# Attention rows of q and k packed into 81 partitions, and the rows of the maxima written by GpSimd's DMAs

## What is computed

```python
mod = silu(c) @ w_adaln + b_adaln            # 6 parts: shift, scale, gate, twice
h   = ln(x) * (1 + scale) + shift
q, k, v = split(h @ w_qkv + b_qkv)           # 16 heads of 9 columns
attn = softmax(q @ k.T * 9 ** -0.5)
x = x + gate * ((attn @ v) @ w_proj + b_proj)
...                                          # layer 0: experts, layer 1: an MLP, with their own ln and gate
```

## Time and profile before

| | |
|---|---|
| median of 3 runs | 464.79 us (460.39 to 464.89) |
| the profiled execution's own time | 465.79 us |
| its span, first to last instruction | 463.9 us |
| PE, DVE, ACT, POOL busy | 84%, 69%, 47%, 18% of the span |
| mean granted TensorE clock | 0.937 of full |

### The profile page before, as it was taken

One profiled execution on the slowest core, in us unless ns is written; L12 is line 12 of the kernel. 1 busy time (PEld: TensorE's weight loads), 2 busy tenths in 40 slices (PEclk: granted clock), 3 DMA queues, 4 the chain that ended last, 5 costly groups with the idle time before them and its releaser, 6 DMA issues.

```text
span 463.9 us, 5953 instructions
## 1 busy us (share of the span) xinstructions
PE 390.6 (84%) x1938; PEld 167.9 (36%) x1938; DVE 321.0 (69%) x837; ACT 216.8 (47%) x428; POOL 85.7 (18%) x95
## 2 busy tenths in 40 slices
PE   1616592689999999899999998998998999998897
PEld 0102220112333332337676663651332333322464
DVE  7797283989889888352716852789797788881653
ACT  1113320157777668752243333124676677687421
POOL 5999945990000000000000000000000000000000
PEclk9999955569999999999999999996999999999999
DMA  6000775124741300000000024300023300000001
GB/s 171 1 0 9 177 182 132 34 81 126 205 131 50 81 1 3 0 1 0 2 0 1 0 76 128 104 2 0 1 70 114 102 27 2 0 3 0 1 0 52
DMA packets 19470, 24.05 MB, mean 52 GB/s; under 512 B 5652, under 2 KB 16088, under 8 KB 19116
## 3 DMA queue, kind: packets, MB, share of 16 engines
q1 hardware_dynamic: 15008, 21.47, 16.4%
q0 software_dynamic: 3040, 1.62, 1.7%
q10 hardware_dynamic: 1392, 0.59, 0.4%
HBM read 19.38 MB, written 4.14 MB: 51 GB/s over the span
## 4 chain that ended last, share of the span: by engine, by line
PE 62%; DVE 16%; DMA 8%; issue 5%; SPq 4%; ACT 4%; DVEq 0%; ACTq 0%
PE bank L1243 12%; PE bank L1121 12%; PE bank L1258 10%; PE bank L1267 8%; PE bank L1221 8%; DVE nmax L938 6%; DMA Qs<-qk_parts 4%; SPq L475 2%; PE bank L1168 2%; DMA qk_parts<-prob 2%; ACT prob L1072 2%; PE bank L1285 2%; PE bank L1224 2%; DVE mpart L739 2%; DMA w<-in_L_cond_b_adaln_dram 1%
## 5 line engine op out<-in xcount | busy, mean ns | idle before, releaser
L938 DVE TENSOR_REDUCE nmax<-bank 128x1 f32<-128x512 f32 x256 | 165.2, 682 | 35.9 <-PE bank L1258 35.1
L1072 ACT ACTIVATE prob<-bank 128x512 f32<-128x512 f32 x256 | 135.5, 602 | 44.1 <-PE bank L1267 43.5
L1258 PE MATMUL bank<-Ks,Qs 96*128 96x512 bf16 x256 | 103.9, 419 | 19.6 <-DMA Qs<-qk_parts 13.1
L1267 PE MATMUL bank<-Qs,Ks 98*128 98x512 bf16 x256 | 98.3, 397 | 5.4 <-ACT prob L1072 4.2
L1121 PE MATMUL bank<-prob,Va 128*32 128x512 f32 x512 | 71.7, 633 | 0.2
L1258 PEld LDWEIGHTS bank<-Ks,Qs 96*128 96x128 bf16 x256 | 25.1, 100 | 91.6 <-DVE nmax L938 48.7
L1243 PE MATMUL bank<-w,big 128*128 128x144 f32 (+1 forms) x320 | 52.5, 305 | 0.2
L1061 ACT ACTIVATE big<-bank 128x512 f32<-128x512 f32 (+1 forms) x46 | 27.0, 597 | 47.0 <-PE bank L1224 46.9
L1243 PEld LDWEIGHTS bank<-w,big 128*128 128x128 f32 (+1 forms) x320 | 42.6, 188 | 10.6 <-DVE y L904 2.6
L1267 PEld LDWEIGHTS bank<-Qs,Ks 98*128 98x128 bf16 x256 | 25.2, 100 | 36.9 <-ACT prob L1072 16.5
L1221 PE MATMUL bank<-hTb,w 128*128 128x512 f32 x72 | 37.0, 594 | 0.0
(11 more groups left out here) (155 smaller groups left out, 452.6 us busy)
## 6 DMA issues: line engine op xcount, KB each, us to landing
Ks<-qk_parts SPq DMA_DIRECT2D x30, 108.0 KB
Qs<-qk_parts SPq DMA_DIRECT2D x90, 36.0 KB
qk_parts<-prob SPq DMA_DIRECT2D x6, 384.0 KB, 4.7
Ks<-qk_parts SPq DMA_DIRECT2D x6, 324.0 KB
Qs<-qk_parts SPq DMA_DIRECT2D x18, 108.0 KB
mod<-modulation SPq DMA_DIRECT2D x5, 288.0 KB, 4.1
w<-in_L_cond_w_dram SPq DMA_DIRECT2D x3, 432.0 KB, 5.4
w<-in_L_cond_w_dram SPq DMA_DIRECT2D x4, 288.0 KB, 3.6
```

Of the source, the lines that this page charges most:

```text
L938: V.tensor_reduce(nmax[:, half, odd * NT + k:odd * NT + k + 1], bank[:, :], AX.X, ALU.max, negate=True).then_inc(s_free, 1)
L1072: A.activation(probs[:, k % 2, j, :], bank[:, :], ACT.Exp, scale=SCALE).then_inc(t_free, 1)
L1258: M.matmul(bank[:, :], Qs[b][0:MROW, h_, k4 * P:(k4 + 1) * P], Ks[b][0:MROW, h_, :], start=True, stop=True).then_inc(s_full, 1)
L1267: M.matmul(bank[:, :], Ks[b][0:SROWS, h0 + k4, k * P:(k + 1) * P], Qs[b][0:SROWS, h0 + k4, :], start=True, stop=True).then_inc(t_full, 1)
```

## The change

- **Rows.** MROW becomes 81: the two rows of the maxima and of ones follow the parts at once (SROWS = 83), there are no zero rows, and all fills of GpSimd for Qs and Ks go away, with the semaphore `buf_ready`. The matmuls are 81 and 83 rows deep.
- **Ones.** DVE sets two partitions of `prob` to one (`onesb`), and two DMAs of ACT's queue spread them over rows 81, 82 of Ks[0] and Ks[1] (64 KB in all). ACT waits for both (`ones_in`) before stage qkv of n = 0.
- **Order of rows.** The rows of Ks are in the order (column, part), and Qs' are at stride 3, so that a piece takes 3 DMAs for Qs with 27 partitions each in place of 9.
- **Pieces.** Batch 0 has three pieces: heads 0 to 3, 4 to 7, 8 to 15.
- **Buffers.** `qkf[1]`, `qkp[1]` lie in Qs[1] in place of prob, so that ACT doesn't wait for `qk_out[0]` before qkv of n = 1, and the first slot waits for `qk_out[0]`, not `qk_out[1]`.
- **Maxima.** For n = 0 the 8 DMAs of mT stay on SP, the other 24 go to GpSimd's queue, behind all its splits.
- **GpSimd.** Va[1] is filled at the start, behind the loads for qkv0. The splits are cut into steps of at most 576 columns (HID).
- **Stages.** ("ada", 1, 0) moves ahead of the first qkv, and (1, 1), (1, 2) and the second turn behind it.

```diff
-MROW = 96
+MROW = PAIRS
...
-    s = [("ada", 0, 0), ("ln", 0, 0), ("ada", 0, 1), ("ada", 0, 2), ("turn", 0, 0, "a"), ("ln", 0, 1),
-         ("qkv", 0, 0, 0, QKV), ("turn", 0, 1, "a"), ("ada", 1, 0), ("ada", 1, 1), ("qkv", 0, 1, 0, QKV), ("ada", 1, 2)]
+    s = [("ada", 0, 0), ("ln", 0, 0), ("ada", 0, 1), ("ada", 0, 2), ("turn", 0, 0, "a"), ("ada", 1, 0),
+         ("ln", 0, 1), ("qkv", 0, 0, 0, QKV), ("ada", 1, 1), ("ada", 1, 2), ("turn", 0, 1, "a"), ("qkv", 0, 1, 0, QKV)]
...
-PIECES = (((0, G), (G, NH)), tuple((h, h + G) for h in range(0, NH, G)))
+PIECES = (((0, G), (G, 2 * G), (2 * G, NH)), tuple((h, h + G) for h in range(0, NH, G)))
...
+def m_landed(pair):
+
+    return (pair % 4, 16 * (pair // 4 + 1)) if 2 * pair < NH else (pair % 4, 16 * ((pair - NH // 2) // 4 + 1))
...
+        onesb = prob[0:MPARTS, 0:N // 2].bitcast(BF16)
+
         qkf, qkp = [], []
-        for place in (prob, prob, prob, big):
+        for place in (prob, Qs[1][:, :, :].rearrange("p h n -> p (h n)").bitcast(F32), prob, big):
...
                     lo, hi = PIECES[b][piece]
-                    width, cols, done = (hi - lo) * N, slice(lo * N, hi * N), qk_in[n][piece]
-                    src = parts[1].rearrange("j (d h) n -> (j d) (h n)", h=NH)[:, cols]
-                    for r in range(0, PAIRS, HD * PARTS):
+                    cols, done = slice(lo * N, hi * N), qk_in[n][piece]
+                    src = parts[1].rearrange("j (d h) n -> d j (h n)", h=NH)[:, :, cols]
+                    for i_ in range(PARTS):
+                        r = HD * PARTS * i_
                         sp.dma_start(Ks[b][r:r + HD * PARTS, lo:hi, :], src).then_inc(done, 16)
-                    for i_ in range(PARTS):
-                        src = parts[0, i_].rearrange("(d h) n -> d (h n)", h=NH)[:, cols]
-                        for r in range(HD * PARTS * i_, HD * PARTS * (i_ + 1), HD):
-                            sp.dma_start(Qs[b][r:r + HD, lo:hi, :], src).then_inc(done, 16)
+                    src = parts[0].rearrange("i (d h) n -> (i d) (h n)", h=NH)[:, cols]
+                    for j in range(PARTS):
+                        sp.dma_start(Qs[b][j:PAIRS:PARTS, lo:hi, :], src).then_inc(done, 16)
...
             load_raw("qkv0")
+            link(G_.memset(Va[1][:, :, :, :], 0.0))
+            G_.memset(Va[1][:, :, :, HD:HD + 1], 1.0).then_inc(v_ready[1], 1)
...
-            for k, (name, last) in enumerate((("proj0", "gate"), ("w1", "w1"), ("qkv1", "fc1"))):
-                a = WCOLS[name][0]
-                split_weights(a, sum(WCOLS[last]) - a).then_inc(w_split, 1)
+            for name, last in (("proj0", "gate"), ("w1", "w1"), ("qkv1", "fc1")):
+                a, end = WCOLS[name][0], sum(WCOLS[last])
+                for at in range(a, end, HID):
+                    done = split_weights(at, min(HID, end - at))
+                done.then_inc(w_split, 1)
+
+            for i, stage in enumerate(SCHED):
+                pair = turns_pair(stage)
+                if pair is not None and 2 * pair >= NH:
+
+                    n, h = 2 * pair // NH, 2 * pair % NH
+                    pool.wait_ge(t_free, T_AT[i + 1])
+                    if n >= B:
+                        pool.wait_ge(t_full, scores_ended(n - B))
+                    pool.dma_start(Qs[n % B][MROW:SROWS, h:h + 2, :], mT[:, pair % 2, :]).then_inc(m_pool[pair % 4], 16)
...
+            act.wait_ge(ones_ready, 1)
+            for b in range(B):
+                act.dma_start(Ks[b][MROW:SROWS, :, :],
+                              onesb.unsqueeze(1).to_broadcast([MPARTS, NH, N])).then_inc(ones_in, 16)
...
-                    if n and first == 0:
+                    if n == 0:
+                        act.wait_ge(ones_in, 16 * B)
+                    if n > 1 and first == 0:
                         act.wait_ge(qk_out[n - 1], 4 * 16)
...
-                        act.wait_ge(qk_out[1 if n0 == 0 else B], 4 * 16)
+                        act.wait_ge(qk_out[n0], 4 * 16)
```

35 lines of the change are left out of this document (13 added, 22 removed).

## The result

The kernel with the change takes 440.12 us (median of 4, 439.02 to 443.79), the kernel before in the same session 463.45 us (460.39 to 464.89): ratio 0.9519, 95% interval 0.9438 to 0.9599. So the change gains 23.3 us where 34 were forecast, and 440 lies at the upper edge of the range. The profiled execution took 441.05 us with a span of 439.2, 24.7 less than before.

A forecast was written before the change was run, and what follows sets the result against it. Before the slots, DVE and GpSimd's fills shut each other out, then waits followed; the slots were PE-bound. Terms -16.0 + 1.2 - 2.0 - 1.9 - 7.9 - 5.0 - 2.5 = -34.1 us gave 431 us, range 423 to 441.

The forecast's parts named there:

- Fills and ones: Without GpSimd's fills, qkv of n = 0 starts at 23.1 us, not 39.17: -16.0; loading the ones costs +1.2.
- Parts to DRAM: In layer 0, the parts' way to DRAM takes 5.0 us, not 7.0, with GpSimd's weight loads mostly over: -2.0.
- First piece: First piece of n = 0 takes 5.3 us, not 7.2, with six issues in 2.15 us: -1.9.
- the term for the transfer: In the first piece, 3.7 us for 648 KB at 175 GB/s, plus 1.0 until first packet and 0.6 at the end.
- Layer 1: PE's waits for first pieces of n = 2 and n = 3 each lose 0.9 to 1.3 us, clock dip partly spared: -2.5.
- Second piece and mpart: Layer 0: smaller pieces remove the second piece's wait, -7.9; shorter GpSimd splits cut waits of DVE's mpart casts, -5.0.
- GpSimd's 24 DMAs at nothing: Maxima pairs on GpSimd's queue land 2.2 us after 0.5 us issues, within the 4.2 us margin: no cost.
- rival 1: Maxima on GpSimd's queue reach the slots late: some late, 437 us, chance 0.10; all late, 487 us, chance 0.03.
- Rival 2: Backlog of the nine DMA engines delays the first slot's maxima to 64 us: +3, so 434 us; chance 0.12.
- Rival 3: New copy shapes use three engines, not nine, so a piece takes 11 us: 456 us; chance 0.03.
- Rival 4: PE stays at the high clock through layer 0's units and first slots: 425 us; chance 0.17.

## Why the prediction was wrong in size

- **Fills and ones: right.** -14.8 forecast, -16.1 at qkv. The two runs on the fills show both cause and size. PE's first product came at 10.27 and not 9.86, and at 9.89 to 10.47 in the other runs, which all write the ones; so these cost 0 to 0.6 of the 1.2 allowed.
- **Parts to DRAM: right** (-2.0, -2.4).
- **First piece: the step that failed.** "Six issues take 2.15" took 0.36 us an issue from the plain rows and gave it to copies of another shape; they take 0.69 to 0.75 each, 4.7 to 5.0 us for six. The first piece of n = 0 got 0.2 us longer in place of 1.9 shorter. The run with the first Q copies on a second queue shows that even with issues of 2.3 us it is 5.9 to 6.8 and not 5.3, so the term for the transfer was too small as well.
- **Layer 1: the same step, and the clock.** -2.5 forecast, +2.7 measured: 5.2 of the 9.4 us. The first piece of n = 2 takes 7.2 us and not 6.1 (279.50 to 285.58 before), that of n = 3 7.0 and not 6.6, so that the waits grew by 1.0 and 0.5 us where 0.9 to 1.3 were to go from each. The longer wait of n = 2 is followed by a low clock (0.72 from 260 to 266) that the kernel before did not have there (1.7 us of lead), and that of n = 3 by a longer one than before (1.5). With plain rows the piece of n = 2 took 1.2 us less, and the fall behind it was gone; but at the first slots the low clock was then 10 us long and not 3.4, and the lead won by it was lost again.
- **The first slots of layer 1: luck.** No term held them. The clock falls there in every kept trace: for 3.4 us in that of the changed kernel, for about 7 in four runs and for about 10 in the kernel before and in the other fourteen. The 2.0 us of lead that came back there stand in the 24.7, and no run shows that the change brings them.
- **Second piece and mpart: right in sum** (-12.9 forecast; the lead grows from 17.4 to 29.9), but the first has the wrong cause. The prediction gave -7.9 to the pieces of 4, 4 and 8; the runs give 1.3 to 1.9 to them and the rest to the fills. The splits are worth 6.4 at the first product with Va where 5.0 were taken.
- **The clock of the first slots of layer 0 and SP's late pair** cost 1.2 and 1.25 us that no term held. The pair is rival 1 on SP's queue; on GpSimd's the same wait came, so its price was real (5.2 us from issue to use) and its reach two pairs.
- **GpSimd's 24 DMAs at nothing: right** within what can be told, by the run with all pairs on SP's queue.
- **Rivals.** Rival 2, the backlog, did not occur: PE's first product with the maxima starts at 62.61 us without a wait for a DMA. Rival 3 does not hold for this shape; its 11 us came with the repeated source. Rival 4, PE staying at the high clock, did not occur, and no run made it occur whole. With the waits filled the clock was low for 20 us of layer 0 in place of 34, and the lead over the changed kernel was 4.8 us at the eighth slot, 0.9 of it from the first unit and 1.0 from the pair that is late there; the 6.6 us at the end have layer 1 in them too, so that their nearness to the 6 it was priced at proves nothing.
- The other differences (1.3 more at qkv, 0.9 less at the third chunk, 0.4 each at parts and units) close the sum: 2.1 + 5.2 + 1.2 + 1.25 + 0.9 - 1.3 - 0.4 + 0.4 = 9.35, the 9.4 but for rounding.

Open: how the transfer of a piece divides among the engines; no view shows single engines. Why the clock of the units falls in some executions in spite of the added matmuls, and what sets how long it is low at the first slots of layer 1. And the slow third chunk of qkv.

## What to carry to other kernels

A merged DMA is not fewer issues of the same price: read the issue time for that very shape, or count it as unknown with both ends, and try a repeated source by itself before relying on it. When a long operation of GpSimd that nobody waits for lies beside DVE's small copies, take it out first; it also moves everything that is queued behind it, and may be the cause of a wait 40 us later. A wait of PE has two prices, its own length and the low clock behind it, and work without a reader can be the cheapest cure of the second. Before a low clock is put down to a change, look whether it only moved: here layer 1 was at the low level for about 14 us before and after.

## What the runs showed of the hardware

- SP's issue of three copies of 108 KB into 27 partitions each: 1.0 us for plain rows; 2.3 to 2.5 where the source has a third dimension; 2.15 where the destination takes every third partition, and 2.2 where the source repeats nine rows three times. Nine plain ones of 36 KB take 3.2.
- GpSimd's fills of 32 partitions x 4096 words take 3.5 us, and DVE's copy of 128x64 beside them up to 3.53 in place of 0.19, though neither waits for the other by a semaphore.
- A copy whose source repeats nine rows three times landed much later than one of 27 rows of the same size: a piece took 11.1 and not 6 to 7 us.
- The granted clock behind PE's wait for the piece of n = 2: waits of 1.23, 1.69 (twice) and 1.98 us were followed by 1.00, waits of 2.12, 2.65, 2.68, 2.71, 2.85, 3.34, 3.74, 3.93 and 6.87 us by 3.4 or 6.8 us at 0.50. At n = 3 it fell for 3.4 us behind a wait of 1.97 us too, so the length of the wait alone does not decide.
- At the first slots of layer 1, where PE's waits for DVE and ACT are 1.23 us at most in the traces of before and after, it was low for 3.4 to 10.3 us in every kept trace.
- GpSimd issued the Q copies that SP issues in 0.69 us in 0.50 to 0.55, and ran ahead of SP's queue where both issued at once: its nine copies were issued by 253.8 us, SP's nine by 256.3.
